# Chunk loop of a gated delta layer: eight loads instead of 32 for the block inversion, another order of SP's loads, and one bank, one copy and one update at inverse level 1

## The reference

```
S_f = fd_t * S_f;  S_s = sd_t * S_s
err_f = v_t - k_t @ S_f;  err_s = v_t - k_t @ S_s
S_f += b_t * outer(k_t, err_f);  S_s += b_t * outer(k_t, err_s)
S_f, S_s = cap(S_f + rf * S_s), cap(S_s + rf * S_f)
o_t = fg_t * (q_t @ S_f) + sg_t * (q_t @ S_s)
```

## Time and profile before

| | us |
|---|---|
| median of 3 runs | 3196.78 (3194.24 to 3200.65) |
| profiled execution, its own time | 3194.22 |
| busy PE / PEld | 2731.8 / 1857.6 |
| busy DVE / ACT / POOL | 2355.7 / 1636.0 / 1359.8 |

### The profile page before, as it was taken

One profiled execution on the slowest core, in us unless ns is written; L12 is line 12 of the kernel. 1 busy time (PEld: TensorE's weight loads), 2 busy tenths in 40 slices (PEclk: granted clock), 3 DMA queues, 4 the chain that ended last, 5 costly groups with the idle time before them and its releaser, 6 DMA issues. The chain is left out here.

```text
span 3192.4 us, 69022 instructions
## 1 busy us (share of the span) xinstructions
PE 2731.8 (86%) x24597; PEld 1857.6 (58%) x24613; DVE 2355.7 (74%) x4311; ACT 1636.0 (51%) x4014; POOL 1359.8 (43%) x2167
## 2 busy tenths in 40 slices
PE   0889996749999999999999999999576688888888
PEld 0654444647777777777777777777574552222223
DVE  7968888937878588685877858766597467777775
ACT  0469996834444444344443434444385445555555
POOL 1112222115656556565665656656474214211111
PEclk9989997969999999999999999999798779999999
DMA  2026657851222313313223132222386212111111
GB/s 61 1 96 245 242 237 242 281 105 35 78 50 61 82 39 79 70 40 84 58 60 69 39 84 65 53 64 77 109 288 202 84 37 44 31 21 23 25 23 28
DMA packets 463053, 288.40 MB, mean 90 GB/s; under 512 B 378323, under 2 KB 422931, under 8 KB 453907
## 3 DMA queue, kind: packets, MB, share of 16 engines
q1 hardware_dynamic: 453494, 254.57, 29.3%
q10 hardware_dynamic: 4608, 16.78, 1.7%
q0 software_dynamic: 4608, 12.59, 1.2%
HBM read 153.83 MB, written 129.99 MB: 89 GB/s over the span
## 5 line engine op out<-in xcount | busy, mean ns | idle before, releaser
L2514 DVE TENSOR_REDUCE mx<-banks 128x2 f32<-128x1024 f32 (+3 forms) x384 | 358.2, 956 | 107.4 <-PE banks L1958 76.2
L2219 ACT ACTIVATE probs<-banks 128x1024 f32<-128x1024 f32 (+3 forms) x384 | 306.2, 810 | 247.2 <-PE banks L1980 230.0
L1744 POOL TENSOR_SCALAR_AFFINE_SELECT probs<-probs 128x256 f32<-128x256 f32 x256 | 104.0, 407 | 524.9 <-ACT probs L2219 524.6
L869 POOL TENSOR_SCALAR xc<-xc,halves 128x64 f32<-128x64 f32 (+1 forms) x256 | 193.9, 758 | 286.7 <-DVE xc L1358 274.1
L1182 ACT COPY xs<-banks 64x128 f32<-64x128 f32 (+1 forms) x384 | 113.4, 295 | 307.7 <-PE banks L1003 306.1
L1837 PE MATMUL banks<-wproj,xnT 128*128 128x512 f32 x512 | 264.8, 599 | 1.7 <-DVEq L495 0.6
L1168 ACT COPY ssm<-banks 16x64 f32<-16x64 f32 (+2 forms) x896 | 215.8, 241 | 57.1 <-PE banks L972 45.0
L1207 ACT COPY ah<-banks 128x768 f32<-128x768 f32 x128 | 102.2, 798 | 269.1 <-PE banks L1038 269.1
L1038 PE MATMUL banks<-stk,tw 128*128 128x192 f32 x1024 | 219.0, 361 | 0.5 <-DVE tw L1363 0.5
L1980 PE MATMUL banks<-q_less,k_parts 64*128 64x512 bf16 (+3 forms) x768 | 133.4, 344 | 83.2 <-DVE mx L2514 62.1
L876 POOL TENSOR_TENSOR ag<-ah,gt_sb 128x512 f32<-128x512 f32 x128 | 162.2, 1267 | 93.3 <-ACT ah L1207 93.1
(11 more groups left out here) (360 smaller groups left out, 6589.4 us busy)
## 6 DMA issues: line engine op xcount, KB each, us to landing
proj_s<-prj SPq DMA_DIRECT2D x32, 2048.0 KB, 6.8
qkv_t<-proj_s SPq DMA_DIRECT2D x32, 1536.0 KB
ka<-proj_s ACTq DMA_DIRECT2D x32, 512.0 KB, 5.0
mem_s<-o_sb SPq DMA_DIRECT2D x32, 512.0 KB, 2.6
om<-mem_s SPq DMA_DIRECT2D x32, 512.0 KB, 3.9
om<-proj_s SPq DMA_DIRECT2D x32, 512.0 KB, 4.9
nblk_s<-ssa POOLq DMA_DIRECT2D x32, 256.0 KB, 4.1
blk_s<-res SPq DMA_DIRECT2D x16, 512.0 KB, 4.1
```

Of the source, the lines that this page charges most:

```text
L869: pool.tensor_scalar(inverse_of(k, lv + 1)[:, :, w:2 * w], inverse_of(k, lv), halves[:, lv, 1:2], None, ALU.mult).then_inc(half_set, 1)
L2219: act.activation(probs[:, s % 2, :, at:at + w], slot_of((kind, s, k))[:, :, 0:w], ACT.Exp, scale=D1 ** -0.5).then_inc(b_read, 1)
L2514: dve.tensor_reduce(mx[:, s % 2, c, :, t:t + 1].rearrange("p e a -> p (e a)"), slot_of((kind, s, k))[:, :, 0:w], AX, ALU.max).then_inc(a_r ...
```

## The change

- `nblk_s` gets the shape (part, row, tile of the part, head, column), so that one DMA per block number j loads all four tiles of a part: 8 loads instead of 32, and `nb` is laid out (row, tile, column).
- The inversion of parts 2 to 7 begins one group after the part before instead of two (`PART_AT`).
- In SP's loop the inverse of a part is stored before tile i - 2 is, and the wait for it to land moves behind the loads of tokens, right and left factors.
- At level 1 both halves' products and updates lie in bank 0 of the slot; ACT copies them with one instruction of 128 partitions and DVE updates with one. Level 2 is written out and stays as it was.

```
-        PART_AT = 2
+        PART_AT = (2, 2, 1, 1, 1, 1, 1, 1)
...
         def products(k, lv, b):
             at = (0, 256)[lv - 1]
-            return slot4(k)[b][:, at:at + 4 * (SUB << lv)]
+            return slot4(k)[0][:, at:at + 4 * (SUB << lv)]
...
-                    for t in range(PT):
-                        sp.dma_start(nb[j:P:NB, t, :].rearrange("h (s o) -> h s o", o=SUB), nblk_s[PT * c + t, q, part_, :, part_].rearrange("s h o -> h s o")).then_inc(nb_in, 16)
+                    sp.dma_start(nb[j:P:NB, :].rearrange("h (n o) -> h n o", o=SUB), nblk_s[c, rows, :, :, part_].rearrange("s t h o -> h (s t) o")).then_inc(nb_in, 16)
...
             for i in range(2, T):
+                c = i // PT
+                if i % PT == 0:
+                    store_part(c)
                 store_tile(i - 2)
                 sp.wait_ge(av_mm, 4 * i - 4)
                 sp.wait_ge(s_new, 4 * i - 4)
-                c = i // PT
-                if i % PT == 0:
-                    store_part(c)
-                    sp.wait_ge(inv_out, 32 * (c + 1))
-                load_tile(i)
+                load_tokens(i)
+                load_right(i)
+                load_left(i)
+                if i % PT == 0:
+                    sp.wait_ge(inv_out, 32 * (c + 1))
+                load_blocks(i)
+                load_ends(i)
                 if i % PT == 0 and c + 1 < T // PT:
                     load_part(c + 1)
...
-                for out_, rows, right in quarters(lv) if lv else ():
-                    last = act.copy(xs[right, k % 2, 0:4 * (SUB << lv)], products(k, lv, out_)[right, :])
+                if lv == 1:
+                    last = act.copy(xs[:, k % 2, 0:4 * (SUB << lv)], products(k, lv, 0))
...
+                if lv == 1:
+                    last = dve.scalar_tensor_tensor(out=inverse_of(k, 2)[:, :, 0:w], in0=inverse_of(k, 1), scalar=halves[:, lv, 0:1],
+                                                    in1=updates(k, lv, 0).rearrange("p (h t) -> p h t", t=w), op0=ALU.mult, op1=ALU.subtract)
...
-                        q -= PART_AT
+                        q -= PART_AT[part]
```

More of the change, by code:

```diff
@@ L87, in layer_kernel @@
         vnorm_s = dram("vnorm_s", (H0, B * L))
-        nblk_s = dram("nblk_s", (T, NB // 2, 2 * SUB, H0, 2 * SUB))
+        nblk_s = dram("nblk_s", (8, P, T // 8, H0, 2 * SUB))
         blk_s = dram("blk_s", (T, 3, H0, NB, SUB, SUB))
@@ L607, in layer_kernel @@
         inv_mem = res[:, :, :].rearrange("p t d -> p (t d)")
-        nb = inv_mem[:, 0:PT * SUB * SUB].rearrange("p (t n) -> p t n", t=PT)
+        nb = inv_mem[:, 0:PT * SUB * SUB]
         tb = inv_mem[:, PT * SUB * SUB:2 * PT * SUB * SUB].rearrange("p (t n) -> p t n", t=PT)
@@ L680, in load_part @@
                 for j in range(NB):
-                    q, part_ = j // 2, slice(SUB * (j % 2), SUB * (j % 2) + SUB)
-                    for t in range(PT):
-                        sp.dma_start(nb[j:P:NB, t, :].rearrange("h (s o) -> h s o", o=SUB), nblk_s[PT * c + t, q, part_, :, part_].rearrange("s h o -> h s o")).then_inc(nb_in, 16)
+                    rows, part_ = slice(SUB * j, SUB * j + SUB), slice(SUB * (j % 2), SUB * (j % 2) + SUB)
+                    sp.dma_start(nb[j:P:NB, :].rearrange("h (n o) -> h n o", o=SUB), nblk_s[c, rows, :, :, part_].rearrange("s t h o -> h (s t) o")).then_inc(nb_in, 16)
             def store_part(c):
@@ L824, in chunk_pool @@
                 pool.wait_ge(ss_kept, 8 * i + 8)
-                pool.dma_start(nblk_s[i].rearrange("q r h o -> (q r) (h o)"), ssa[:, n, :, :].rearrange("p h o -> p (h o)")).then_inc(nblk_out[n], 16)
+                pool.dma_start(nblk_s[i // PT, :, i % PT, :, :].rearrange("p h o -> p (h o)"), ssa[:, n, :, :].rearrange("p h o -> p (h o)")).then_inc(nblk_out[n], 16)
                 if i == ZERO_AT:
@@ L1180, in keep_lower @@
                         last = act.copy(xs0[rows, k % 2, :, own], span4(k, 2, 2).rearrange("p (e c) -> p e c", e=2)[rows, :, own])
-                for out_, rows, right in quarters(lv) if lv else ():
-                    last = act.copy(xs[right, k % 2, 0:4 * (SUB << lv)], products(k, lv, out_)[right, :])
+                if lv == 1:
+                    last = act.copy(xs[:, k % 2, 0:4 * (SUB << lv)], products(k, lv, 0))
+                if lv == 2:
+                    right = HALVES[1]
+                    last = act.copy(xs[right, k % 2, 0:4 * (SUB << lv)], products(k, lv, 0)[right, :])
                 last.then_inc(x_set[lv], 1)
@@ L1251, in begin_inverse @@
             def begin_inverse(c):
-                dve.wait_ge(nb_in, 16 * NB * PT * (c + 1))
+                dve.wait_ge(nb_in, 16 * NB * (c + 1))
                 if c:
@@ L1258, in inverse_row @@
             def inverse_row(c, s_):
-                rows, lower_ = tb.rearrange("p t (s o) -> p t s o", o=SUB), nb.rearrange("p t (s o) -> p t s o", o=SUB)
+                rows, lower_ = tb.rearrange("p t (s o) -> p t s o", o=SUB), nb.rearrange("p (s t o) -> p t s o", t=PT, o=SUB)
                 sh = [P, PT, s_, s_]
@@ L1359, in keep_update @@
                                                     in1=updates0(k).rearrange("p (h t) -> p h t", t=w), op0=ALU.mult, op1=ALU.subtract)
[L1360 to L1366, removed]
+                if lv == 1:
+                    last = dve.scalar_tensor_tensor(out=inverse_of(k, 2)[:, :, 0:w], in0=inverse_of(k, 1), scalar=halves[:, lv, 0:1],
+                                                    in1=updates(k, lv, 0).rearrange("p (h t) -> p h t", t=w), op0=ALU.mult, op1=ALU.subtract)
+                if lv == 2:
+                    right = HALVES[1]
+                    last = dve.tensor_scalar(tw[right, k % 2, :, 0:w], updates(k, lv, 0)[right, :].rearrange("p (h t) -> p h t", t=w), -1.0, None, ALU.mult)
                 last.then_inc(tw_set[lv], 1)
```

6 lines of the change are left out of this document (removed).

## The result

The changed kernel takes 3105.52 us, median of 4 runs (3103.32 to 3107.53), against 3197.09 (3194.24 to 3200.65) for the kernel before on the same chip: ratio 0.9713, 95% interval 0.9696 to 0.973, so 91.6 us less where 110 were forecast. The profiled execution took 3105.23 us.

A forecast was written before the change was run, and what follows sets the result against it. Bounds: PE's in-order stream with few waits per step, and a DMA wait about every sixteenth step. 60 us from groups plus 49.7 from waits made 110: 3084 us profiled, 3086 median; range 3074 to 3122, own range 3074 to 3102.

The forecast's parts named there:

- Part 1: Inversion's level 1, one bank, copy and update: 0.47 us less in each of 128 groups, 60 us in all.
- the 0.18 goes: Level 1: PE's 0.18 us wait for ACT's copy, before the weight load of update 1 (L1017), disappears.
- end of 23 us: Low end for the level-1 merge: nothing but the 0.18 us per group arrives; the high end was 68 us.
- Part 2: SP's new order: opening tiles of parts 2 to 7 come on time; c = 1 keeps 0 to 3 us, taken 0.5.
- six stalls: PE's waits at L963 for the opening tiles of parts 2 to 7, all forecast to go with the slow clock.
- Part 3: Eight loads instead of 32 in SP's queue: 13 us of issue, ends 6 and 22; 12.2 us of late tiles go.
- late second tiles: Long steps three groups after a part's opening tile, in four parts; with what follows them 12.2 us, forecast to go.
- even 22 us would do no harm: Aside on SP's eight loads: with no issue time saved, SP would still be free at 1100.
- the 49.7: Microseconds to be gained from waits in the chunk loop: 32.0 + 6.0 - 0.5 + 12.2.
- (a): Rival, SP's loads: tiles still come late, half of the 50 us of waits stays, 3109 us; chance 8%.
- (b): Rival, level 1: next wait, for ACT or DVE, swallows the gain; only 23 us arrive, 3121 us; chance 7%.
- (c): Rival, level 1: halves' matmuls cannot overlap into one bank, up to 34 ns more each, 3223 us; chance 4%.

## Why the prediction came out as it did, point by point

**Direction: right; mechanism: right but for one link.** 3105.5 lies in the range of 3074 to 3122, just above the own range of the forecast (3074 to 3102). The waits came out within 1 us of their sum partly by luck, as told under the sum.

**Part 1, the step that failed: "the 0.18 goes".** It was to help bring 0.53 to products 2 and 0.47 to the step, 60 us; the level brought 0.37 and 0.36, 44.5 us. The update's 0.35 arrived but for a few hundredths (0.295 alone). The copy's 0.18 brought 0.045. The wait of the earlier trace rows was read as the distance to go, but behind it stood a second lower bound that no idle row showed: PE itself leaves 0.12 us between the last weight load of the states (64x128) and the first of a 64x64 group. The kernel after shows it at both places, with no waiting for another engine. How it comes about can be read from the rows shown of that kernel. The states' first load (993.22) starts 0.07 before the end that the profile models for the products' last matmul (992.64 + 0.65 = 993.29), 0.05 behind the last load. Update 1 (993.86) starts 0.07 before the modelled end of the states' last matmul (993.22 + 0.71 = 993.93), 0.12 behind the last load. So across either change of shape the next load keeps one distance to the last matmul, and the gap is as long as that matmul makes it: 32 columns in the products, 128 in the states. With all shapes 64x64, the loads of products and states interleave instead. The Trainium skill says in "TensorEngine Tiling (Array Packing)", Key Properties, that changing the tiling mode makes TensorE drain; these rows agree with it. That alike shapes remove the gap in front of update 1 and products 2 is not shown, since there ACT and DVE come last in the kernel with 64x64 states; and that it is the drain and not another cost of the 128-wide group was not separated by a run. The forecast's end of 23 us (only the 0.18) is the mirror of what came: it kept the smaller term and doubted the larger.

**Its other links held.** Partitions cost nothing: 266 and 347 ns for the merged pair, by form in the kernel after. Against the earlier trace rows:

```profile
L1361 DVE SCALAR_TENSOR_TENSOR xc<-xc,halves,banks 128x128 f32<-128x128 f32 x128 | 44.5, 347 | 69.4 <-PE banks L1014 68.8
L1179 ACT COPY xs<-banks 128x128 f32<-128x128 f32 x128 | 34.1, 266 | 265.3 <-PE banks L1000 265.3
```

**Part 2: right for six parts, wrong in size for part 1.** The six stalls went. Part 1 was to keep 0 to 3 us, taken 0.5, and kept 6.3 of step from 3.36 of idle. Two things failed: the tile's loads were given the 26 us of an ordinary tile and took 29.1 beside the stores of the inverse, and the cost was read as the idle time alone, though the forecast itself says ahead of its parts that a stall costs about twice that.

**Part 3: the gain was right, its reason half.** The late second tiles are gone. The eight loads take 5.5 to 6.8 us of issue, where 13 were forecast: some 0.7 us each, near the low end (0.8 each) that the forecast named and did not take. The statement that even 22 us would do no harm was wrong by 8.6 us of loop. It cost nothing because the loads were short.

One of the four late second tiles in the forecast was none. At part 6 of the kernel before (steps of 13.50 and 12.15) the transposes of the second tile waited for nothing, and the clock fell two us later (timeline of PE, then a window with the columns of the earlier trace rows):

```profile
1924.91 0.66 PE L963 MATMUL banks<-ident,qkv_t 128*128 128x128 f32 x4
```

```profile
1927.00:1931.00 4.00, 4.00 (x18) 3.30 (x16) 2.80 (x9) 1.01 (x2) 1.26 (x4) 0.57 0.00 0
```

So 1.65 of the 12.2 us were no wait for a load.

**Sum.** 60 became 44.5 (15.5 missing); the 49.7 became 48.9, since what the forecast left alone (8.5 us of start, end and inversion) fell to 3.5 and made up for part 1; the ends of the kernel took 4.2. 109.7 - 15.5 - 0.8 - 4.2 = 89.2, against 89.1 of span. That the 8.5 fell was luck as far as the forecast goes: some 3.3 of it were two more pairs of long steps like the one just shown (13.13 and 12.20 in mid-loop, 13.34 and 12.35 at the start), which it neither named nor priced. The kernel after has none; no run tests why.

**Rivals.** (a) Tiles late in half the places: no, one in seven; it would have come true with `PART_AT` left at 2. (b) The level's gain swallowed by the next wait, for ACT or DVE: 45 of 60 arrived, and the one that swallowed the rest was PE, which the rival did not name. (c) One bank slows the matmuls of the halves: refuted, 0.54 for sixteen weight loads before, after and in the kernel with the copy alone (0.55 in one row). The Trainium skill's "TensorEngine Tiling (Array Packing)", Gotcha 1: PSUM Pressure, says that different row tiles cannot access the same PSUM bank simultaneously; no run shows a cost of it here. The Trainium skill's "PSUM — Partial Sum Buffer", on bank collisions, narrows the conflict to one bank and the same quadrant of 32 partitions. The trace agrees in so far as the halves, which write different quadrants of one bank, are as fast as in two banks.

## What to carry to other kernels

When a wait is removed, the gain is the distance to the second-latest release, and the engine's own floor is one of them: look for gaps between groups of matmuls of different shape that no other engine accounts for. Keep neighbouring groups of small matmuls in one shape of the array: that was worth 0.25 us a step here. Where a DMA queue must store a result before it can load, finish the producer earlier; the reordered queue with the late producer left all seven tiles late.

## What the runs showed that was not expected

The clock can fall without a long wait. In the kernel with 64x64 states and no merge, about a dozen stretches of two to four steps take 12.0 to 13.6 us a step with no wait for a DMA in the loop. One of them has steps of 12.90, 13.58 and 12.22 us, from 778.66 to 817.37 (windows, columns as in the earlier trace rows):

```profile
782.00:794.00 12.00, 11.34 (x131) 8.70 (x129) 8.56 (x20) 3.88 (x12) 7.84 (x13) 0.86 0.17 19
794.00:806.00 12.00, 11.34 (x131) 9.39 (x131) 9.91 (x22) 4.54 (x14) 6.71 (x12) 0.86 0.01 2
806.00:818.00 12.00, 11.33 (x144) 8.86 (x142) 8.63 (x21) 5.00 (x17) 7.14 (x13) 1.00 0.18 58
```

PE is busy 94% of these windows, yet the granted clock is 0.86 in two of three. The kernel before has three such pairs (13.34 and 12.35, 13.13 and 12.20, 13.50 and 12.15), the one with SP's program alone two, the one with the copy alone two, the one with 32 loads in the new order three. The kernels with the merged update have none that stands apart from a late tile or the start of the loop. The merge, which takes small waits out of every step, may thus also keep the clock up; but the kernel with the eight loads alone, without the merge, has none either. It is a pattern over single executions, and no run was made to test it.

Two groups of matmuls on the same 64x64 pieces of the array overlap their weight loads: 16 and 16 loads in 0.88 us of the kernel with 64x64 states (983.52 to 984.40), where 16 and 8 of the larger took 1.11 (992.63 to 993.74).
